# Convolution stage of a fused decoder: the split on two row tiles of TensorE, the join on two column tiles, and relayouts between 8 and 128 partitions instead of 16 and 128

## The reference, cut to what matters

```python
k = shift_k(k) + k_D * k        # shift_k: convolution of k with k_kernel along the sequence, by rfft with n = 2L
kv = k * v
y = irfft(rfft(kv, n=2L) * rfft(ssm_kernel, n=2L), n=2L)[..., :L] + kv * D
```

## Time and profile before

| | us |
|---|---|
| median of three runs | 5086.95 (5080.97 to 5093.71) |
| the profiled execution | 5107.29 |
| its span | 5105.5 |
| PE busy in the span | 4847.5 |
| DVE busy | 2858.2 |
| ACT busy | 1662.8 |
| POOL busy | 1812.5 |
| convolution stage, about 2160 to 2645 | 485 |
| PE busy in it | 433.53 |

### The profile page before, as it was taken

One profiled execution on the slowest core, in us unless ns is written; L12 is line 12 of the kernel. 1 busy time (PEld: TensorE's weight loads), 2 busy tenths in 40 slices (PEclk: granted clock), 3 DMA queues, 4 the chain that ended last, 5 costly groups with the idle time before them and its releaser, 6 DMA issues. The chain is left out here.

```text
span 5105.5 us, 124764 instructions
## 1 busy us (share of the span) xinstructions
PE 4847.5 (95%) x49200; PEld 3357.9 (66%) x49200; DVE 2858.2 (56%) x4880; ACT 1662.8 (33%) x2033; POOL 1812.5 (36%) x1684
## 2 busy tenths in 40 slices
PE   9999999989999999989979999789999999999998
PEld 4444445658887756534334566478889888888788
DVE  4244236766654345466752576566666666666665
ACT  1001005544333210045431444233333333333333
POOL 1001004645554411022232234444445444444443
PEclk9999999989999999999989999899999999999999
DMA  1000011141111233397866111146666677889996
GB/s 61 9 33 25 9 58 56 59 117 41 41 34 34 75 109 107 119 245 221 216 210 256 49 51 51 50 118 222 222 221 223 222 248 258 306 304 318 312 316 201
DMA packets 422050, 743.99 MB, mean 146 GB/s; under 512 B 119905, under 2 KB 203622, under 8 KB 415284
## 3 DMA queue, kind: packets, MB, share of 16 engines
q1 hardware_dynamic: 293376, 661.44, 36.9%
q0 software_dynamic: 48448, 76.66, 6.7%
q10 hardware_dynamic: 79988, 2.67, 1.0%
HBM read 559.39 MB, written 107.88 MB: 131 GB/s over the span
## 5 line engine op out<-in xcount | busy, mean ns | idle before, releaser
L3562 PE MATMUL ex_ps<-ex_w,ex_xT 128*32 128x256 f32 x20992 | 1228.3, 380 | 31.4 <-DVE ex_w L3463 22.3
L3562 PEld LDWEIGHTS ex_ps<-ex_w,ex_xT 128*32 128x32 f32 x20992 | 1027.9, 110 | 178.1 <-DVE ex_w L3463 30.7
L3463 DVE COPY ex_w<-ex_shelf 128x4096 f32 x328 | 748.8, 2283 | 329.2 <-PE ex_ps L3562 161.2
L3520 ACT ACTIVATE ex_w<-ex_shelf 128x4096 f32 x164 | 595.0, 3628 | 809.5 <-PE ex_ps L3574 687.8
L3574 PE MATMUL ex_ps<-ex_w,ex_hT 128*32 128x256 f32 x10496 | 650.3, 379 | 9.1 <-ACT ex_w L3520 4.1
L3426 POOL DMA_INDIRECT out<-ex_y,ex_ix_out x164 | 306.6, 1869 | 824.4 <-DVE ex_xT L3450 350.4
L3409 POOL DMA_INDIRECT ex_x<-moe_xn,ex_ix x328 | 528.6, 1612 | 137.4 <-issue 99.1
L3574 PEld LDWEIGHTS ex_ps<-ex_w,ex_hT 128*32 128x32 f32 x10496 | 521.9, 110 | 83.8 <-issue 17.9
L2575 POOL DMA_DIRECT2D cv_vt<-cv_v x256 | 134.1, 530 | 376.6 <-ACT cv_v L2675 372.3
L634 PE MATMUL at_ps<-at_xT,at_kT 128*128 128x512 f32 (+3 forms) x640 | 239.3, 529 | 1.6 <-ACT at_kT L528 1.6
L634 PEld LDWEIGHTS at_ps<-at_xT,at_kT 128*128 128x128 f32 x640 | 116.7, 190 | 121.8 <-issue 109.1
(11 more groups left out here) (367 smaller groups left out, 8065.9 us busy)
## 6 DMA issues: line engine op xcount, KB each, us to landing
ex_shelf<-L_ffn_w SPq DMA_DIRECT2D x128, 2048.0 KB
ex_shelf<-L_ffn_wo SPq DMA_DIRECT2D x64, 2048.0 KB
cv_gt<-cv_g SPq DMA_DIRECT2D x320, 128.0 KB
cv_vt<-cv_v POOLq DMA_DIRECT2D x256, 128.0 KB, 3.3
ff_x<-x SPq DMA_DIRECT2D x16, 1024.0 KB
ex_raw_x<-slot_token ACTq DMA_DIRECT2D x656, 0.5 KB
at_low<-x SPq DMA_DIRECT2D x8, 1024.0 KB
x<-at_acc SPq DMA_DIRECT2D x8, 1024.0 KB, 4.2
```

Source lines behind the costliest of these rows:

```text
L3463: dve.tensor_copy(w_s[n][:, :], pick(shelf[n], buf)).then_inc(w_set[n].sem, 1)
L3520: act.activation(w_s[2][:, :], pick(shelf[2], buf), ACT.Copy).then_inc(w_set[2].sem, 1)
L3562: mm = pe.matmul(ps[r * LANES:(r + 1) * LANES, which, hh * FL:(hh + 1) * FL], xT[:, p % 2, k, hh * LANES:(hh + 1) * LANES], wu[which][:, k ...
```

## The change

- **Split**: each unit now uses one half of the contraction, 64 partitions, and yields all 128 outputs. Units with even u take partitions 0 to 63, odd u 64 to 127, so consecutive units stand on two row tiles and in two banks. The input is loaded so that it fits: partition 64*l + (j, k) holds rows (j, l, k). ACT puts unit u to `g1[:, u % 2, u // 2 * 2 : ...]`.
- **Join**: the two matmuls of a unit no longer accumulate; each takes one l of vt, contracts over all 128 partitions and yields 64 outputs, the first to partitions 0 to 63 of the bank, the second to 64 to 127.
- **Relayouts**: residue r lies on the 8 partitions base_row(r) + 4x, base_row(r) = 32*(r % 4) + r // 4. A spread DMA moves 8 partitions of 16 KB to 128 of 1 KB, a gather the reverse. Numbers and bytes of both are as before.
- **Waits**: spread(n+1, 0) and spread(n+1, 1) are both issued in slot (n, 1), each after unit 7 has been taken; ACT waits for both halves of the spread before it takes unit 0.
- **Loads and stores**: two DMAs of 64 partitions each, the semaphores count 32. The tables in `transform_tables` are permuted, with unused parts left zero.

```diff
+def base_row(r):
+    return 32 * (r % 4) + r // 4
...
 def half_rows(v, hh, first=0):
     at = hh * (v.shape[0] // (D // CW)) + first
-    return v[at:at + UN * P, :].rearrange("(p i) d -> p i d", i=UN)
+    return v[at:at + UN * P, :].rearrange("(j l k i) d -> l j k (i d)", l=2, k=2, i=UN)
...
-                r = 4 * (q % 2) + a
-                eng.dma_start(vt[PLACE[r]:P:UN, e % 2, q // 2], v1[:, q % 2, a, :]).then_inc(vt_in[e % 2][q], 16)
+                eng.dma_start(vt[base_row(4 * q + a):base_row(4 * q + a) + 29:4, e % 2], v1[:, q % 2, a, :]).then_inc(vt_in[e % 2][q], 16)
...
-                sp.dma_start(xin[:, l % 2], src).then_inc(x_in[l % 2], 16)
+                for k in range(2):
+                    sp.dma_start(xin[64 * k:64 * k + 64, l % 2], src[k]).then_inc(x_in[l % 2], 16)
...
-                sp.wait_ge(*taken(unit_at["split", n, 4 * q + 3]))
+                sp.wait_ge(*taken(unit_at["split", n, 7]))
                 st.plain(sp)
-                for r in range(UN):
-                    sp.dma_start(gt[:, n % 2, UN * q + r, :], g1[PLACE[r]:P:UN, q]).then_inc(gt_in[n % 2][q], 16)
+                for r in range(UN * q, UN * (q + 1)):
+                    sp.dma_start(gt[:, n % 2, r, :], g1[base_row(r):base_row(r) + 29:4]).then_inc(gt_in[n % 2][q], 16)
...
-                    if q < 2 and n + 1 < NST:
-                        spread(n + 1, q)
+                    if q == 1 and n + 1 < NST:
+                        spread(n + 1, 0)
+                        spread(n + 1, 1)
...
-                    if n and u % 4 == 0:
+                    if n and u == 0:
                         prior = n - 1
-                        act.wait_ge(gt_in[prior % 2][u // 4], 128 * (prior // 2 + 1))
-                    act.activation(g1[:, u // 4, 2 * (u % 4):2 * (u % 4) + 2, :].rearrange("p i d -> p (i d)"), bank, ACT.Copy).then_inc(aux_act, 1)
+                        for half in range(2):
+                            act.wait_ge(gt_in[prior % 2][half], 128 * (prior // 2 + 1))
+                    act.activation(g1[:, u % 2, u // 2 * 2:u // 2 * 2 + 2, :].rearrange("p i d -> p (i d)"), bank, ACT.Copy).then_inc(aux_act, 1)
...
-                    rows = here[:, 2 * (u % 4):2 * (u % 4) + 2, :].rearrange("p i d -> p (i d)")
-                    i = pe.matmul(bank, split[:, u // 4, :], rows, start=True, stop=True)
+                    mine = slice(64 * (u % 2), 64 * (u % 2) + 64)
+                    rows = here[mine, u // 2 * 2:u // 2 * 2 + 2, :].rearrange("p i d -> p (i d)")
+                    i = pe.matmul(bank, split[mine, 0, :], rows, start=True, stop=True)
...
-                    for q in range(2):
-                        rows = vt[:, e % 2, q, 2 * u:2 * u + 2, :].rearrange("p i d -> p (i d)")
-                        i = pe.matmul(bank, join[:, q, :], rows, start=q == 0, stop=q == 1)
+                    for l in range(2):
+                        rows = vt[:, e % 2, l, 2 * u:2 * u + 2, :].rearrange("p i d -> p (i d)")
+                        i = pe.matmul(ps[64 * l:64 * l + 64, a % 2, :], join[:, 0, 0:64], rows, start=True, stop=True)
```

More of the change, by code:

```diff
@@ L2416, in transform_tables @@
     by_row = np.arange(P).reshape(UN, P // UN)[np.argsort(PLACE)].T.reshape(P)
-    split = split.reshape(P, 2, P)[:, :, by_row]
-    join = join.reshape(2, P, P)[:, by_row]
+    halved = np.arange(P).reshape(RES, 2, 2).transpose(1, 0, 2).reshape(P)
+    by_slot = np.array([[base_row(r) + 4 * x for x in range(UN)] for r in range(RES // 2)]).reshape(P)
+    narrow = np.zeros((2, RES, 2, RES, 2, 2))
+    for n in range(RES):
+        for k in range(2):
+            narrow[:, :, k, n, :, k] = split[:, 0, n, :, 0]
+    split = np.zeros((P, 2, P))
+    split[:, 0, by_slot] = narrow.reshape(P, P)
+    fwd = fwd.reshape(2, 2, 2, 2, UN, RES // 2, 2, RT).transpose(0, 1, 3, 2, 4, 5, 6, 7)
+    narrow = np.zeros((RES, 2, 2, RES, 2))
+    for k in range(2):
+        narrow[:, :, k, :, k] = join[:, :, 0, :, 0]
+    join = np.zeros((2, P, P))
+    join[0, by_slot, 0:P // 2] = narrow.reshape(P, P // 2)
+    inv = inv.reshape(4, RT, RES // 8, 2, 2, 2, 2, 2, UN).swapaxes(6, 7)
     return (split.reshape(P, 2 * P).astype(f), fwd.reshape(P, RES * RT).astype(f),
@@ L2442, in early @@
     def early(sp):
-        sp.dma_start(st.xin[:, 0], half_rows(kkT, 0)).then_inc(st.x_in[0], 16)
+        for l in range(2):
+            sp.dma_start(st.xin[64 * l:64 * l + 64, 0], half_rows(kkT, 0)[l]).then_inc(st.x_in[0], 16)
         for i, v in enumerate((kd, dd)):
@@ L2447, in early @@
         sp.dma_start(st.fwd.rearrange("p a b c -> p (a b c)"), tables_d[1]).then_inc(st.tab_in[1], 16)
-        sp.dma_start(st.xin[:, 1], half_rows(k_in, 0)).then_inc(st.x_in[1], 16)
+        for l in range(2):
+            sp.dma_start(st.xin[64 * l:64 * l + 64, 1], half_rows(k_in, 0)[l]).then_inc(st.x_in[1], 16)
         sp.dma_start(st.inv.rearrange("p a b c d -> p (a b c d)"), tables_d[2]).then_inc(st.tab_in[2], 16)
@@ L2585, in load_x @@
                 src = half_rows((kkT, ssT)[conv], hh) if b is None else seg_rows(k_in, n)
-                sp.dma_start(xin[:, l % 2], src).then_inc(x_in[l % 2], 16)
+                for k in range(2):
+                    sp.dma_start(xin[64 * k:64 * k + 64, l % 2], src[k]).then_inc(x_in[l % 2], 16)
             def load_v(n):
                 if half_of[n]:
-                    sp.wait_ge(stored[slot_of[n]], 16 * half_of[n])
+                    sp.wait_ge(stored[slot_of[n]], 32 * half_of[n])
                     st.plain(sp)
-                sp.dma_start(vb[:, slot_of[n]], seg_rows(v_in, n)).then_inc(v_in_s[slot_of[n]], 16)
+                for k in range(2):
+                    sp.dma_start(vb[64 * k:64 * k + 64, slot_of[n]], seg_rows(v_in, n)[k]).then_inc(v_in_s[slot_of[n]], 16)
             def spread(n, q):
@@ L2606, in store @@
                 st.plain(sp)
-                sp.dma_start(seg_rows(y_out, n), vb[:, slot_of[n]]).then_inc(stored[slot_of[n]], 16)
+                for k in range(2):
+                    sp.dma_start(seg_rows(y_out, n)[k], vb[64 * k:64 * k + 64, slot_of[n]]).then_inc(stored[slot_of[n]], 16)
             spread(0, 0)
@@ L2623, in _ @@
             for p in range(SEGS):
-                sp.wait_ge(stored[p], 16 * NH)
+                sp.wait_ge(stored[p], 32 * NH)
         @block.gpsimd
@@ L2683, in tap @@
                 l = load_of[n]
-                dve.wait_ge(x_in[l % 2], 16 * (l // 2 + 1))
+                dve.wait_ge(x_in[l % 2], 32 * (l // 2 + 1))
                 dve.tensor_tensor(xin[0:1, l % 2, 0, :], xin[0:1, l % 2, 0, :], gain[0:1, hh, conv, :], ALU.add).then_inc(tapped, 1)
@@ L2720, in take @@
                 if u == 0:
-                    dve.wait_ge(v_in_s[slot_of[n]], 16 * (half_of[n] + 1))
+                    dve.wait_ge(v_in_s[slot_of[n]], 32 * (half_of[n] + 1))
                 o = vb[:, slot_of[n], 2 * u:2 * u + 2, :].rearrange("p i d -> p (i d)")
@@ L2747, in aux @@
                         elif n in load_of:
-                            pe.wait_ge(x_in[load_of[n] % 2], 16 * (load_of[n] // 2 + 1))
+                            pe.wait_ge(x_in[load_of[n] % 2], 32 * (load_of[n] // 2 + 1))
                         else:
```

## The result

The changed kernel takes 5266.27 us (median of 4 runs, 5264.38 to 5277.87), the kernel before beside it 5086.25 (5080.97 to 5093.71): a ratio of 1.0358, 95% interval 1.0338 to 1.0377. It is 180 us slower. 142 were forecast, and 5266 lies inside the range of 5100 to 5310.

What follows compares the result with a forecast made beforehand. PE bounds the kernel before, DMA close behind; after the change the ring does. Seventeen periods of 30.5 and two of 25 against 416.3 us give +152, less 10: +142 on 5087, so 5229 us, range 5100 to 5310.

Steps and rivals of the forecast that it cites:

- the ring: Convolution steps: with g1 one generation, period = split phase + T, 30.5 us; likeliest case, on eight engines, chance 0.70.
- Split phase: Split units of a step, from the first eviction until unit 7 is out: 8.8 us, against 9.1 before.
- Clock: PE after standing: the lower 1.2 GHz level adds 0 to 2.5 us to the split phase, taken as 1.5.
- Eight engines: Spread relayouts with 8 partitions on one side: served by eight DMA engines, 11.1 to 18.6 us of data a step.
- rival of sixteen engines: Spread relayouts: sixteen engines serve them after all, issue sets T, period 22 to 24, 5093 us; chance 0.08.
- Gathers starving in the split phase: Rival: gathers meet the loaded engines, the copy of v waits, period about 37, 5340 us; chance 0.15.
- PE as the bound: Rival: PE's 19.5 us a step outlasts the ring, shorter join slots pay, 5017 us; chance 0.07.
- T: Spread of a step, from first relayout issue to last landing: 20.2 us, between 13.0 and 26.2.
- I take 15.3: Data time of a step's relayouts within T: 15.3 us, at the cost of steady slots with gathers beside them.
- I take 3: Gathers' addition to T in each step: 3 us, between 0 if hidden and 5.7 if it adds up.
- Edits at no cost: Half loads and stores: 28 more SP issues at 0.51 us, 0.7 a step, hidden; tables and gather count free.
- it gains 10: Stage outside the ring: gains 2 us in the first splits and 8 in the joins behind the last spread.

Runs made afterwards that it cites:

- the tiles alone: Changed kernel with both tables zero-padded to 128x128, so all split and join matmuls run on the whole array: 5290.22 us, ratio 1.0401.
- loads after the landing: Changed kernel with one more SP wait, so a step's loads and stores go out only when all sixteen relayouts have landed: 5255.07 us, ratio 1.0332.
- ring alone: Kernel before with only the changed kernel's two waits, with whole-array matmuls and relayouts of 16 partitions: 5151.5 us, ratio 1.0132.
- the join part with whole loads: Kernel before with column-tiled joins and gathers onto 8 partitions, loads and stores in one DMA each, split and relayouts as before: 5117.94 us, ratio 1.0011.

## Why the prediction was right, and where it was off

The sign, the ring as the mechanism and the order of size were right. **Ring**: the seventeen full periods are 31.7 against 30.5; blocks of sixteen and a DMA share of 0.64, as named beforehand. **Split phase** 10.4 against 8.8 + 1.5. **Clock**: 0.50, the 1.2 GHz level, behind the waits, as in the earlier trace rows. The run with half of the relayouts on POOL's queue tells what it costs: its PE gets the full clock in most split phases. One of that run, and the one shown above of the changed kernel (windows):

```profile
2467.99:2476.39 8.40, 7.07 (x108) 3.05 (x108) 4.64 (x8) 6.37 (x11) 4.68 (x8) 1.00 0.32 84
```

```profile
2443.53:2454.55 11.02, 9.69 (x108) 3.90 (x108) 3.70 (x6) 6.38 (x11) 2.65 (x6) 0.69 0.49 109
```

The same 108 records take 2.6 us less of PE; on the mean of all steps the phase is 8.5 at a clock of 0.96 and 10.4 at 0.73, so the two terms were nearer 8.4 and 2. **Join slot** 1.94 against 1.85. **Eight engines**: 50.8% and 72 updates; so the rival of sixteen engines falls. The Trainium skill's rule (DMA: Bandwidth & Descriptors, Why a DMA increments its semaphore by 16 and not by 1), that the slowest dimension sets the count of engines, holds for this on-chip relayout as for ff_sc. By the same section the issuing sequencer writes at once what the engines left out would have added, which fits the ninth update of each relayout. That the count of engines also sets the relayout's pace was taken over from other transfers, and the run on two queues speaks against it. **Gathers starving in the split phase**: ACT waits 16.0 us for cv_vt in all, so that rival falls too. **PE as the bound** falls with a T of 21.

Three of the signs that were named did not come as named. ACT's unit 0 waits 4.7 us a step for cv_gt (89.2 over 19; the longest is 7.5), not 6 to 10. PE stands 13 us a step (247 over 19), not 6 to 10. And L2753 (now L2778) is busy 143.5 us for 161.4, not half; only the join's L2761 (now L2786) comes near it, 65.2 for 120.2. With whole-array splits at the same place in the ring, in the run of the tiles alone, it is 193.9, so the tiles do their part, and the low clock takes some of it back (2.56 us for two units in the step shown above, 1.61 for the same two at full clock in the run with two queues).

In the seventeen full periods T came out as 21.2 for 20.2. That it is so near is luck: two errors nearly cancel.
- "I take 15.3" for the data was too much: 12.8 (0.80 each), and 2.8 from there to the last landing for "1.9". This adds up to 15.6, the T of the one step measured with neither gathers nor loads beside it (loads after the landing, second step). Eight engines are full, but their packets are shorter than the 58.4 engine-us a MB of the earlier trace rows made them.
- "I take 3" for the gathers was too little: by the run with a quarter of them some 6.7 in a step with all its gathers, above even the bound of 5.7; and on the mean of the seventeen steps 5.0 (T of 20.6 with the loads out of the way, less 15.6). So their time on an engine adds up, and they land later themselves. The view of their line in the changed kernel, against the earlier trace rows:

```profile
DMA to landing us min/median/max: 2.7/5.0/16.9
```

Three terms account for the 42 us between the forecast for the stage and the +184 there:
- **Seventeen full periods**, 31.7 for 30.5: 20 us, nearly all of it T.
- **The first two periods**, 28.3 for 25: 7 us. The 25 stood there without working, and was below the prediction's own terms: without gathers these give 8.8 + 1.5 + 17.2 = 27.5. The other step that failed is "Edits at no cost": a half load was held to cost 0.51 us of SP's time, and was not priced on the engines at all. Whole loads make these two periods 26.7 on average, which is half of the 7 us, and win back 22 us in the whole kernel.
- **Outside the ring**, "it gains 10": it lost 5. The first spread now waits for eight units instead of four (9.5 us for 5.3), which the step overlooked, and the joins behind the last spread wait for gathers. The end of the stage in the kernel before and in the changed one:

```profile
2627.11 9.21 PE L2761 MATMUL cv_ps<-cv_vt,cv_join 128*128 128x512 f32 x16 [6.02 <-DMA cv_vt<-cv_v]
```

```profile
2818.90 5.38 PE L2786 MATMUL cv_ps<-cv_vt,cv_join 128*64 128x512 f32 x16 [10.09 <-DMA cv_vt<-cv_v]
```

Sixteen records in 5.38 us for 9.21, behind a wait of 10.09 for 6.02: what PE saves, the wait takes.

Of the 180 us, then: ring alone 63; the tiles give back 24; so, if these add, the layout's DMA side costs some 140 on top of the ring. Inside it the half loads are 22, and the rest is the relayout of 0.80 us and the gathers onto 8 partitions, which the runs part by T (12.8 with 16 partitions, 16.6 with 8, in the two steps without gathers and with whole loads) but not as a sum of their own. No version tried here beats the kernel before; the nearest is the join part with whole loads, at +4.

## What to carry to other kernels

Before a matmul is put on tiles, ask what layout the tiles want and price the relayouts first: here 24 us of gain from the tiles stood against some 200 for the order and the DMAs that they want. When a change makes a buffer one generation where it was two, write out the ring (phase + issue + landing) and compare it with the period of now; it costs even where no engine gets more to do (63 us here). And price a DMA by the partitions of both its sides, loads included: half the partitions is not half the time.

## What was not expected

- A load of 64 partitions runs at half the pace of one of 128 (604 against 313 ns, medians of the packets). Cutting all loads and stores of the stage in two costs 31 us in the kernel before, 22 in the changed one, and some 50 beside gathers onto 8 partitions.
- A DMA issued behind another one slows it: in the first spread the last relayouts' packets go from 53 ns to 92 and then 120 on average once the x load behind them begins; in the second, T is 18.1 with the loads and 15.6 without.
- Eight engines moved relayouts nearly as fast as sixteen: 1.58 MB in 10 us against 1.73 with 16 partitions in the run of the ring alone (where the last landing is only some 2 us behind the last issue), so the form alone made T 16.6 for 12.8, and not twice as long.
- Half of the relayouts on POOL's queue filled all sixteen engines and moved hardly more (176 GB/s for 158), so it is not a want of engines that holds these relayouts back.
